# Fewer, larger transfers in an attention and expert layer: the maxima of a head pair in one, the routing weights of two experts in one

## The reference

```python
h = _layernorm(x)
q, k, v = (jnp.einsum('bsd,hde->bhse', h, W) for W in (Wq, Wk, Wv))
scores = jnp.where(causal, jnp.einsum('bhse,bhte->bhst', q, k) / 8, -jnp.inf)
heads = jnp.einsum('bhst,bhte->bhse', jax.nn.softmax(scores, -1), v)      # then b s (h e)
y = h + heads @ Wo
x = x + ((y - mean(y)) * rsqrt(var(y) + 1e-3) * gamma + beta)

t = _layernorm(x)                                    # all B * S tokens
probs = softmax(t @ gate_w.T)
top_w, top_idx = top_k(probs, 8); top_w /= sum(top_w)
comb = sum(one_hot(top_idx, 32) * top_w[..., None], axis=1)               # tokens x experts
for guw, dw, w_e in zip(gate_up_w, down_w, comb.T):
    g, u = split(t @ guw.T)
    acc = acc + (u * silu(g) @ dw.T) * w_e[:, None]
x = x + acc
```

## Time and profile before

| | |
|---|---|
| median of 3 runs | 1748.65 us (1747.98 to 2051.43) |
| profiled execution, its own time | 1747.59 us |
| its span, first to last instruction | 1745.7 us |
| mean granted TensorE clock | 0.991 |
| busy: PE, PEld | 1633.9 us (94%), 1113.7 us (64%) |
| busy: DVE, ACT, POOL | 1462.4 (84%), 1404.4 (80%), 1403.9 us (80%) |
| mean busy share of the 16 DMA engines | about 50% |

### The profile page before, as it was taken

The page is one execution under the profiler, slowest core; times in us unless marked ns, Lnnn a source line. Parts: engine busy times, 40 slices in busy tenths (PEclk is TensorE's granted clock), DMA queues, the critical chain, the costliest instruction groups (busy, mean ns, idle before and its releaser), DMA issues.

```text
span 1745.7 us, 56980 instructions
## 1 busy us (share of the span) xinstructions
PE 1633.9 (94%) x21209; PEld 1113.7 (64%) x21209; DVE 1462.4 (84%) x4484; ACT 1404.4 (80%) x2364; POOL 1403.9 (80%) x1164
## 2 busy tenths in 40 slices
PE   3799999999999999999999999999999999999868
PEld 1366766666666666666666666666676666667655
DVE  7999889797887978879797887979889797887757
ACT  2799888797887879788797888879788787888752
POOL 4477997888879788887888979788897888889880
PEclk9999999999999999999999999999999999999999
DMA  5554554646455464544646454473645546435423
GB/s 181 128 122 106 145 136 123 166 106 158 104 132 129 106 178 110 142 115 115 174 106 159 110 140 124 104 186 95 158 117 133 139 106 165 123 109 138 112 79 105
DMA packets 219444, 226.26 MB, mean 130 GB/s; under 512 B 27041, under 2 KB 185249, under 8 KB 218913
## 3 DMA queue, kind: packets, MB, share of 16 engines
q1 hardware_dynamic: 219168, 222.61, 49.8%
HBM read 82.53 MB, written 5.24 MB: 50 GB/s over the span
## 4 chain that ended last, share of the span: by engine, by line
PE 61%; SPq 8%; DVE 8%; DMA 6%; POOL 6%; issue 5%; ACT 5%; POOLq 0%; ACTq 0%; DVEq 0%
PE bank_r L389 15%; PE bank_s L389 12%; PE bank_v L389 8%; PE bank_g L389 8%; PE bank_u L389 8%; PE bank_x L389 7%; SPq L321 3%; POOL p_lo L1497 2%; DMA expert_room<-comb_rows 2%; SPq L335 2%; SPq L311 1%; SPq L312 1%; POOL expert_room L1512 1%; DMA xt<-in_x 1%; SPq L310 1%
## 5 line engine op out<-in xcount | busy, mean ns | idle before, releaser
L1497 POOL TENSOR_TENSOR p_lo<-p,p_hi 128x1280 f16<-128x1280 f32 x256 | 674.7, 2636 | 149.0 <-ACT p_hi L786 148.2
L848 ACT ACTIVATE p<-bank_s,back 128x512 f32<-128x512 f32 (+1 forms) x768 | 461.4, 615 | 61.9 <-PE bank_s L389 53.8
L389 PE MATMUL bank_s<-score_ops 128*128 128x62 f16 (+10 forms) x4096 | 405.6, 233 | 20.6 <-DMA score_ops<-rowmaxT 15.3
L389 PEld LDWEIGHTS bank_s<-score_ops 128*128 128x128 f16 x4096 | 278.1, 97 | 192.5 <-issue 46.8
L1512 POOL TENSOR_TENSOR expert_room<-expert_room 128x512 f32<-128x512 f32 x240 | 304.4, 1275 | 34.7 <-DMA expert_room<-comb_rows 17.4
L786 ACT ACTIVATE p_hi<-p 128x1280 f16<-128x1280 f32 x256 | 324.6, 1268 | 7.8 <-PE bank_r L389 2.2
L1516 POOL TENSOR_TENSOR halves<-expert_room,halves 128x512 f16<-128x512 f32 x240 | 276.4, 1162 | 29.0 <-ACT halves L786 27.3
L1124 DVE CUSTOM_DVE_ANT_0 max_junk<-bank_r,mask 128x384 f16<-128x384 f32 (+3 forms) x523 | 232.1, 474 | 36.6 <-PE bank_g L389 16.3
L389 PE MATMUL bank_x<-w_hi,halves 128*128 128x128 f16 x1920 | 199.1, 220 | 2.0 <-POOL halves L1516 2.0
L786 ACT ACTIVATE halves<-expert_room 128x512 f16<-128x512 f32 x240 | 150.1, 625 | 44.8 <-POOL expert_room L1512 32.2
L389 PE MATMUL bank_x<-w_lo,halves 128*128 128x128 f16 x960 | 173.2, 220 | 0.0
(11 more groups left out here) (298 smaller groups left out, 5015.4 us busy)
## 6 DMA issues: line engine op xcount, KB each, us to landing
score_ops<-nat SPq DMA_DIRECT2D x256, 256.0 KB, 3.8
score_ops<-nat SPq DMA_DIRECT2D x512, 128.0 KB, 3.6
expert_room<-comb_rows SPq DMA_DIRECT2D x480, 128.0 KB, 3.0
xt<-in_x SPq DMA_DIRECT2D x16, 256.0 KB, 3.5
xb<-in_x SPq DMA_DIRECT2D x16, 256.0 KB, 4.1
score_ops<-rowmaxT SPq DMA_DIRECT2D x256, 2.0 KB
out_y<-expert_room SPq DMA_DIRECT2D x16, 256.0 KB, 3.4
score_ops<-comb_rows SPq DMA_DIRECT2D x32, 128.0 KB, 3.0
```

Of the source, the lines that this page charges most:

```text
L389: return pe.matmul(dst, lhsT, rhs, start=start, stop=stop, skip_group_check=shared)
L848: act.activation(p32[:, h % P_SLOTS, at:at + cols], bank[score_bank(h, u)][:, 0:cols], ACT.Exp, scale=back[:, SC_SCORE:SC_SCORE + 1]).then ...
L1497: pool.tensor_tensor(p_lo[:, slot, :], p32[:, slot, :], p_hi[:, slot, :], ALU.subtract).then_inc(p_lo_done, 1)
```

## The change

`place_max` issues one transfer for each pair in place of two; `keep_weights` one in place of four; `spread_weights` one for both experts of a step in place of two. The semaphores' counts follow. The lists of all engines, what each step waits for and the tiles stay as they are. In the shapes: a maxima transfer goes from [8, 128] on both sides to 16 partitions of 128 on the side that is read and [2, 8, 128] on the side that is written; the kept weights from [32, 128] to [4, 32, 128] in device memory; the spread weights from a row read 64 times, [64, 512], to [2, 64, 512], the outer count being the two experts, written to 128 partitions.

```diff
@@ place_max
-                    for part in range(2):
-                        at = 16 * k + 8 * part
-                        sp.dma_start(home[part:part + 1], rowmaxT[at:at + 8, :]).then_inc(max_placed[g], 16)
+                    sp.dma_start(home, rowmaxT[16 * k:16 * k + 16, :]).then_inc(max_placed[g], 16)
@@ keep_weights
-                for c in range(C):
-                    sp.dma_start(comb_rows[:, c * P:c * P + P], combT[c * NE:c * NE + NE, :]).then_inc(comb_stored, 16)
+                sp.dma_start(comb_rows.rearrange("e (c p) -> c e p", c=C), combT).then_inc(comb_stored, 16)
@@ spread_weights
-                    sp.wait_ge(comb_stored, 16 * C * (p + 1))
+                    sp.wait_ge(comb_stored, 16 * (p + 1))
                 if p < B - 1:
                     wait(sp, a_lo_done, p * EP + j - RING + 1)
-                for e in range(2):
-                    sp.dma_start(weighed(p, j)[ED * e:ED * e + ED, :],
-                                 comb_rows[2 * j + e:2 * j + e + 1, :].to_broadcast([ED, S])).then_inc(spread_sem(p, j), 16)
+                sp.dma_start(weighed(p, j),
+                             comb_rows[2 * j:2 * j + 2].rearrange("a (b s) -> a b s", b=1).to_broadcast([2, ED, S])).then_inc(spread_sem(p, j), 16)
@@ scores (PE)
-                        pe.wait_ge(max_placed[h // 4], 64 * (m + 1))
+                        pe.wait_ge(max_placed[h // 4], 32 * (m + 1))
@@ copy_maxima (ACT)
-                wait(act, max_placed[(g - 1) % QUADS], 64 * (m + 1) if g else 64 * m)
+                wait(act, max_placed[(g - 1) % QUADS], 32 * (m + 1) if g else 32 * m)
@@ weigh_last (DVE)
-                dve.wait_ge(last_spread[j], 32)
+                dve.wait_ge(last_spread[j], 16)
@@ weigh_unit (POOL)
-                pool.wait_ge(comb_spread[j % RING], 32 * (p * (EP // RING) + j // RING + 1))
+                pool.wait_ge(comb_spread[j % RING], 16 * (p * (EP // RING) + j // RING + 1))
```

## The result

The changed kernel takes 2499.4 us (median of 4 runs, 2497.5 to 2504.7) against 1750.2 us: 1.429 times the time, with an interval of [1.426, 1.433]. The forecast was 2465 us, 2150 to 2740. The profiled execution took 2504.67 us, its span is 2502.9 us against 1745.7: 757.2 us more.

A forecast was written before the change was run, and what follows sets the result against it. It took PE's pace as the bound, busy for 94% of the span. 1747.59 us + 612 for 14 rounds + 42 and 68 for the last two elements gave 2470, less small gains 2465 us; range 2150 to 2740.

The forecast's parts named there:

- Over how many engines: Merged transfers: outermost count sets the DMA engines; new spread over 2, maxima over 2, store over 4.
- A spread's price: Merged spread of 256 KB: 128 KB on each of 2 engines, 5.6 us, bounds 5.2 to 6.6.
- One round: Loop round: 106 us of line in place of 62.3, +43.7; rest unchanged at 38; 612 us over 14 rounds.
- The last two elements: Elements 14 and 15: spreads landing one after another on two engines add 42 and 68 us.
- The small gains: Saved SP issue before maxima and first weights: at most some 33 us; a few us subtracted in the sum.
- Rival (a): Loop: PE's waits overlap the busy two engines, only capacity counts, 119 to 125 us a round; 2070 to 2165 us; chance 0.13.
- Rival (b): Spreads: still dealt over 16 engines, 1715 to 1747 us; chance 0.08 faster, 0.05 within 2%.
- Rival (c): Loop: late units at POOL starve the ring, engines run dry between spreads; 2600 to 2800 us; chance 0.08.
- The forecast's own signs: Profile after: PE's maxima waits near 9 us just behind the first four spreads, some 17 at each of the next two placements.
- The clock: PE: a granted clock that falls in its long waits would add to the forecast; no size given.

The follow-up runs named there:

- two_by_two: Kernel before, nothing merged, but the 64 repeats of each spread written as 2 times 32; 2505.0 us, 1.432 times the kernel before.
- interleaved_all: Changed kernel, all three merges, with a step's two experts interleaved over the partitions so the 64 repeats stand outside; 1709.4 us, 0.978 of the kernel before.
- last_alone: Kernel before with only the last element's spreads merged as in the change; 1813.6 us, 1.035 times the kernel before.
- maxima_act: Changed kernel with the maxima transfers issued by ACT and taken out of SP's queue; 2553.9 us, 1.457 times the kernel before.
- four_engines: Kernel before, nothing merged, but the 64 repeats of each spread written as 4 times 16; 2024.5 us, 1.155 times the kernel before.

## Why the prediction was right

**Over how many engines.** Right: two, two and four, read from the marks, and the cause shown by two_by_two (2505 us without a merge) and interleaved_all (1709 us with all merges).

**A spread's price.** Taken as 5.6 us, bounds 5.2 and 6.6; it is 5.2 us where spreads alone are in the line, the rate of large rows. Among operands it is about 5.8, an estimate: (104.8 - 4 x 4.2 - 1) / 15. A row of 2 KB takes 96 ns on average there and 85 in the last element. So 5.6 was near for the loop and high for the end, between two bounds that both occurred in part.

**One round.** Predicted +43.7 us, 42.4 in the line and none in the rest. The trace shows 104.7 - 62.3 = 42.4 and 45.3 - 38.2 = 7.1, +49.4 in this round; over the 14 rounds 2128.5 us in place of 1465.1, +663 for a predicted +612. Two errors of opposite sign are in it. With the 5.2 us of the last element the sum would give 37.7. The difference is not a line that ran dry: it was never empty, and counting nothing for that was right. Its transfers were slower when mixed, by the 5.8 us above. The first number agrees so well by some luck, since the stretch is counted from issue to issue. The forecast took the landing behind it (about 1 us) as the same, and it is 6.6 us in place of 1.0 (median over the twelve rounds), because SP issues the maxima while the line in front of them still holds. This is most of the 7.1 us by which the rest grew. In the rest `xt` lands late as well (DVE waits 196.6 us for it in 13 places), and the clock is 0.90; the shares of these two were not told apart.

**The last two elements.** Predicted +42 and +68; measured from store to store 112.1 in place of 76.8 us, +35, and from the last store to the end 95.1 in place of 34.4, +61. With 5.2 us for a spread the sum gave +36 and +62, and last_alone +61. The sum closes: 663 + 35 + 61 - 2 (the first store comes 2 us earlier) = 757.

**The small gains.** "At most some 33 us" was too low: 39 us, all from the maxima. The step took PE's and POOL's wait times for the limit, and at 27 placements PE passed the wait with the last mark without being seen idle. The row that held more was the chain's SPq share, 8% or 140 us.

**Rival (a)**, capacity alone, fell by maxima_act: even with the maxima out of the line the round stays at 155 us. It wanted the engines busy all round, and they are not: in the 45.5 us behind the fifteenth spread fewer than two packets are under way for 19.6 us. The reason that I gave against it (maxima with 2.8 us of lead in the same line) was true and not sufficient: it is enough for a loss of 293 us, but the weights' own lateness is enough for all of it. In the forecast "PE can't start those scores without these maxima" was therefore the wrong carrier for the right sum. The forecast's own signs show it too: it wanted waits near 9 us behind the first four spreads and 17 at each of the next two placements, and they are 0, 13.6 and 11.8. The sum came out because the term in it, the time of the line, was the right one, whoever waits for it. That the rest stays at 45 to 49 us and does not overlap with the line is read from the traces; what in the lists (ring, POOL, DVE) holds it there was not taken apart.

**Rival (b)** fell by the marks. **Rival (c)** did not occur: from the first spread to the fifteenth the engines did not run dry. In four_engines they did, for some 8 us a round.

**The clock.** The mean granted clock is 0.864 in place of 0.991, and lower where PE waits more (0.65 in the stretch from 2420 us, where it is busy for 33.4 of 70 us); PE's instructions take 163 us more for it. How much of these is on the path no run tells.

## What to carry to other kernels

Before merging transfers, write down the counts of both sides and look at the outermost: it limits the number of DMA engines, and a merge that puts a 2 in front of 64 repeats makes a transfer of 256 KB take 5.2 us of two engines, where sixteen would take an estimated 0.65 at the same rate; the same bytes with the 64 outside cost nothing. For a transfer of a few KB in front of a waiting engine the opposite holds: two engines instead of eight were harmless, and 1.3 us less issue at 64 places gave 39 us. To price a line in a shared queue, add up what its busiest engine must carry between two points of the schedule, at the rate of mixed traffic. The waits name whoever has the least lead, and taking that one out of the line doesn't help if another in it is nearly as late.

## What the runs showed of the hardware

The outermost count of the source decided even where both counts of the repeats have step 0: 2 x 32, 4 x 16 and 8 x 8 of one row gave 3, 5 and 9 marks where 64 gave 16, so they were not folded.

SP is held when the line is long. In the changed kernel the issue of a spread takes a median of 0.55 us in the loop and 5.1 us for the last element; issue times are least, median and most, in ns:

```profile
L331 SPq DMA_DIRECT2D expert_room<-comb_rows x240: 474/553/5599, 169.7 to 2371.1; - x120
...
L331 SPq DMA_DIRECT2D score_ops<-comb_rows x16: 501/5093/7214, 2410.6 to 2477.0; - x16
```

A transfer of another kind is held as well, here the load of `xb`, which has 16 marks and whose issue took 0.59 us before (start and length in us):

```profile
1277.16 6.49 SPq L300 DMA_DIRECT2D xb<-in_x  x1
```

The last spread is issued at 2477.0 and lands at 2496.4 us, 19.3 us or not quite four spreads later: SP did not get further ahead than that in the whole last element, and what stands behind it in SP's list waits with it.
